# Queries of the cross attention laid out in DRAM as a group's tile has them, loaded by three DMAs a group and stored by three a tile

## The reference, cut to what matters

```python
def _L0_xattn_ref(query, key, value, masked, Wq, Wk, Wv, Wo):     # query: x of shape (4, 1024, 256); key, value: context (4, 77, 256)
    q = split_heads(query @ Wq)                                    # 16 heads of 16
    k = split_heads(key @ Wk)
    v = split_heads(value @ Wv)
    scores = jnp.einsum('bhqd,bhkd->bhqk', q, k) * scale
    scores = jnp.where(masked[:, None, :, :], NEG, scores)
    attn = jax.nn.softmax(scores, axis=-1)
    out = jnp.einsum('bhqk,bhkd->bhqd', attn, v)
    return out.transpose(0, 2, 1, 3).reshape(query.shape[0], -1, EMBED_DIM) @ Wo
```

## Time and profile before

| | us |
|---|---|
| three runs | 1057.42, 1067.87, 1074.19 |
| median | 1067.87 |
| the profiled execution | 1068.38 |
| its span, first to last instruction | 1066.7 |

### The profile page before, as it was taken

One profiled execution on the slowest core, in us unless ns is written; L12 is line 12 of the kernel. 1 busy time (PEld: TensorE's weight loads), 2 busy tenths in 40 slices (PEclk: granted clock), 3 DMA queues, 4 the chain that ended last, 5 costly groups with the idle time before them and its releaser, 6 DMA issues.

```text
span 1066.7 us, 19077 instructions
## 1 busy us (share of the span) xinstructions
PE 1025.8 (96%) x7059; PEld 603.9 (57%) x7108; DVE 722.7 (68%) x1603; ACT 577.6 (54%) x1093; POOL 198.3 (19%) x220
## 2 busy tenths in 40 slices
PE   5999999999999999999999999899999999999998
PEld 4877344444444444444444466444544588888887
DVE  7878887787887787877785387646566365555552
ACT  4785276676766676676675667457556411111110
POOL 6655000000000000000000034101000033333331
PEclk9999699999999999999999999869999999999999
DMA  8696903444443334444400048758673100000001
GB/s 259 207 280 209 177 6 78 82 82 82 82 69 60 65 64 78 86 85 82 81 14 19 10 122 185 174 89 159 117 130 61 33 8 21 20 21 20 20 21 40
DMA packets 82202, 93.27 MB, mean 87 GB/s; under 512 B 14676, under 2 KB 75312, under 8 KB 80573
## 3 DMA queue, kind: packets, MB, share of 16 engines
q1 hardware_dynamic: 79527, 88.85, 38.3%
q10 hardware_dynamic: 2582, 3.20, 1.4%
HBM read 53.55 MB, written 28.80 MB: 77 GB/s over the span
## 4 chain that ended last, share of the span: by engine, by line
PE 77%; DVE 14%; ACT 3%; issue 2%; DMA 2%; SPq 1%; POOL 0%; POOLq 0%; DVEq 0%; ACTq 0%
PE bank L134 20%; PE bank L870 12%; PE bank L837 11%; PE bank L856 9%; DVE pm L767 7%; PE bank L1544 3%; PE bank L1440 3%; PE bank L1430 2%; PE bank L1432 2%; PE bank L1141 2%; PE bank L968 2%; PE bank L860 2%; PE bank L1413 2%; PE bank L842 2%; PE bank L1415 1%
## 5 line engine op out<-in xcount | busy, mean ns | idle before, releaser
L767 DVE TENSOR_REDUCE pm<-bank 128x1 f32<-128x512 f32 (+3 forms) x608 | 356.9, 654 | 86.6 <-PE bank L842 65.6
L814 ACT ACTIVATE prob<-bank 128x512 f32<-128x512 f32 (+1 forms) x608 | 317.5, 584 | 174.0 <-PE bank L860 87.9
L837 PE MATMUL bank<-stk,stq 96*128 96x512 bf16 (+3 forms) x768 | 224.4, 336 | 5.6 <-DVE pm L767 3.2
L856 PE MATMUL bank<-stq,stk 98*128 98x512 bf16 (+3 forms) x768 | 221.5, 328 | 2.7 <-ACT prob L814 0.7
L870 PE MATMUL bank<-prob,va 128*17 128x512 f32 (+3 forms) x1536 | 145.0, 496 | 2.7
L837 PEld LDWEIGHTS bank<-stk,stq 96*128 96x128 bf16 x768 | 68.3, 98 | 134.9 <-DVE pm L767 76.8
L1692 ACT ACTIVATE e_sg<-bank 128x512 f32<-128x512 f32 x48 | 28.7, 598 | 174.4 <-PE bank L134 172.3
L1379 ACT ACTIVATE xprob<-bank 80x512 f32<-80x512 f32 x128 | 73.0, 592 | 73.8 <-PE bank L1432 70.8
L753 POOL TENSOR_TENSOR xres<-xres,bo_b 128x256 f32<-128x256 f32 x32 | 23.2, 724 | 399.2 <-DVE pm L767 204.2
L856 PEld LDWEIGHTS bank<-stq,stk 98*128 98x128 bf16 x768 | 69.1, 98 | 44.7 <-ACT prob L814 9.1
L1609 POOL TENSOR_TENSOR e_ht<-e_hf,e_ht 128x512 fp32r<-128x512 f32 x48 | 62.2, 1296 | 109.9 <-DVE e_ht L1634 109.8
(11 more groups left out here) (183 smaller groups left out, 1354.6 us busy)
## 6 DMA issues: line engine op xcount, KB each, us to landing
qk<-a_parts SPq DMA_DIRECT2D x32, 384.0 KB, 2.8
xq<-c_parts SPq DMA_DIRECT2D x16, 384.0 KB, 2.7
xstq<-xq SPq DMA_DIRECT2D x32, 192.0 KB, 4.2
stq<-qk SPq DMA_DIRECT2D x30, 192.0 KB, 3.9
stk<-qk SPq DMA_DIRECT2D x15, 384.0 KB, 6.4
vs<-a_vst SPq DMA_DIRECT2D x8, 544.0 KB, 3.8
oall<-u_out SPq DMA_DIRECT2D x64, 64.0 KB
xstq<-xq SPq DMA_DIRECT2D x32, 128.0 KB, 4.5
```

The costliest lines, as they stand in the source:

```text
L767: nc.vector.tensor_reduce(pm[:, k, h0:h0 + hb, r], src[:, 0:hb * w].rearrange("p (h w) -> p h w", h=hb), AX, ALU.max).then_inc(s_mxe, 1)
L814: nc.scalar.activation(prob[:, U % NPS, 0:hb * n], bank[STB[U % NSB]][:, 0:hb * n], ACT.Exp).then_inc(s_ex, 1)
L837: mm = nc.tensor.matmul(dst[:, h * w:(h + 1) * w], stq[i][0:R, half, h0 + h, r * P:(r + 1) * P], stk[i][0:R, h0 + h, k0:k0 + w], start=(h ...
L856: mm = nc.tensor.matmul(dst[:, h * n:(h + 1) * n], stk[i][0:RM, h0 + h, kt * P:(kt + 1) * P], stq[i][0:RM, half, h0 + h, q0:q0 + n], start ...
```

## The change

`xq3` gets the order that a group's tile has: for a batch, a half of the features, a part and a number r of the head there are two groups, and for a group 2 halves x 4 heads x 512 queries lie together, 8 KB in one piece. Before, a head's 1,024 queries lay together (2 KB). A load then takes one piece of 8 KB for each partition, and three DMAs fill a tile. The stored tile's rows no longer share one stride for all partitions and parts, so each part has a DMA of its own. The numbers that the semaphores are waited for follow.

```diff
-    xq3 = dram("xq3", (B, KT, 3, P, S), BF16)
+    xq3 = dram("xq3", (B, KT, 3, HD, HP // HG, 2, HG, CH), BF16)
...
                 sp.wait_ge(cs_lo, KT * c + n + 1)
-                sp.dma_start(xq3[b, n, :, :, u * CH:(u + 1) * CH].rearrange("c p s -> p c s"),
-                             cparts[:, u, n]).then_inc(cso[u], 16)
+                for part in range(3):
+                    sp.dma_start(xq3[b, n, part, :, :, u].rearrange("r a h s -> (r a) h s"),
+                                 cparts[:, u, n, part]).then_inc(cso[u], 16)
...
-                        sp.wait_ge(cso[w], 16 * KT)
+                        sp.wait_ge(cso[w], 48 * KT)
                     load_cross(sp, c - 2)
             for w in range(2):
-                sp.wait_ge(cso[w], 16 * KT * B)
+                sp.wait_ge(cso[w], 48 * KT * B)
...
-                need(a, cso[c % 2], 16 * KT * (c // 2))
+                need(a, cso[c % 2], 48 * KT * (c // 2))
...
             for slot, first, number in Q_RUNS:
-                for c in range(2):
-                    sp.dma_start(xstq[i][HD * slot:HD * (slot + number), c],
-                                 xq3[b, i // 2, first:first + number, :, c * 512:(c + 1) * 512]
-                                 .rearrange("c (r h) s -> (c r) h s", h=HP)
-                                 [:, HG * (i % 2):HG * (i % 2 + 1)]).then_inc(xld[i], 16)
+                sp.dma_start(xstq[i][HD * slot:HD * (slot + number)].rearrange("p u h q -> p (u h q)"),
+                             xq3[b, i // 2, first:first + number].rearrange("c r a u h s -> (c r) a (u h s)")
+                             [:, i % 2]).then_inc(xld[i], 16)
...
-                    t.wait_ge(xld[i], 32 * len(Q_RUNS) * (b + 1))
+                    t.wait_ge(xld[i], 16 * len(Q_RUNS) * (b + 1))
```

## The result

The changed kernel took 1067.94 us, the median of 21 runs (1062.14 to 1075.17). The kernel before, in 21 runs beside it, had 1061.04 (20 of them between 1057.42 and 1074.23; one of 3491.92 doesn't move the median). The ratio is 1.0059, with a 95% interval of 1.0042 to 1.0076: slower by 0.6%, about 6 us, clear of noise and well inside 2%. The forecast of 1068 us with "no change beyond 2%" holds. That the figure was hit is luck, two errors that cancel: I added 0.1 us to a median of three runs, 1067.87, that stood 7 us above what more runs of the same kernel give, and the change cost about 6 us.

The account below looks back on a forecast made before the run. TensorE bounds the kernel (77% of the span); DMA waits with the low clock offer 13.5 us. +0.1 (last store) + 0 (earlier stores, issue, bytes, group 7) on 1068.38 gives 1068.5, forecast 1068 us; range 1055 to 1080 for 8 in 10.

Parts of the forecast that it names:

- no change beyond 2%: Whole kernel: time stays within about 2% (21 us) of the kernel before, given 93 in 100.
- the bytes of the loads: Query loads: 8 KB runs flow no faster than 1 KB runs; 0 us, ends 2.2 less and 1.2 more.
- Rival (a): Query loads flow faster in long runs, 2.2 us less; idle time and low clock go, 1055 us; 6 in 100.
- Rival (c): Long-run query loads flow slower, 1.2 us more each, 1082 us; with one further low stretch, 1080, together 12 in 100.
- (d): Query loads: the 8 KB runs are cut into short packets again; only SP's issue time is saved, 1068 us.
- the place: Cross stage: TensorE's 2.1 us wait for group 1's maxima row; with the low clock behind it 13.5 us to win.
- the last store: Last query store before group 3's load: third part issued at 676.02, landing at 677.8 to 678.6; +0.1 us.
- a store that ends later holds up nobody: Stores before the last: 12 us more of SP's issue time fits into its 33.4 us of waiting; 0 us.
- The low clock stays: Behind group 1's wait: the 24 us low stretch, costing 11.4 us, remains, as idle time goes from 2.07 to about 2.2 us.
- Rival (b): Clock falls for a shorter time or not at all, with waits as they are; 1057 us; 22 in 100.
- group 7: Group 7's load behind 768 KB of `up_t`, TensorE idle 0.69 us: no change, 0 us, ends -0.7 and +1.2.
- over 1 us at group 7: Sign that the forecast is wrong: a wait for `xstq` of over 1 us at group 7 or later.

Follow-up runs that it names:

- loads3: Kernel before with only the loads changed: three loads a group, 8 KB runs, one store a tile as before; 1059.57 us, ratio 0.9986.
- stores3_flat: Kernel before with only the stores changed: three a tile, old order in DRAM, 128 rows each; 1063.07 us, ratio 1.0028.
- early_after: Changed kernel with group 1's maxima row sent ahead of the wait for the last stores and of group 3's load; 1059.75 us, ratio 0.9992.
- the 67 runs: Later runs of the unchanged kernel before, beside the experiments, two slow ones of 69 left out; on average 1061.4 us.
- base: Kernel before once more, no edit, with every run's granted clock on record; 1058.35 us, ratio 0.9982.
- early_before: Kernel before with only group 1's maxima row sent ahead of the wait for the last stores and of group 3's load; 1059.29 us, ratio 0.9975.
- delay3: Kernel before plus three spare stores of 32 x 4 rows issued between the wait for the last stores and group 3's load; 1063.09 us, ratio 1.0045.
- early_weights: Kernel before with the early maxima row, and `up_t` and `down_t` issued behind a group's query load; 1057.36 us, ratio 0.9982.

## Why the prediction was right, and which steps were wrong

**Right: the bytes of the loads.** Long runs flow as fast as short ones. In the change, group 3's load is first issued at 679.85 and its last 128 KB, issued at about 680.7, landed 6.1 us later:

```profile
xstq<-xq SPq DMA_DIRECT2D x1, 128.0 KB, 6.1
```

That is 6.9 us from first issue to last landing, against 6.7 before and "6 to 7" forecast; `loads3` puts it alone and finds 0.9986. The self-attention stage was the right place to read this price. Rival (a) falls: no run shows a joined load landing sooner. The Trainium skill, page "DMA: Bandwidth & Descriptors", section on rules for kernel authors, speaks for joining small transfers, and the page's fit, which it gives for transfers issued from GpSimd, made an estimated 3.8 us of it; the measured 6.9 us decide against both here. Rival (c), slower long runs, falls too, and (d) by the packets.

**Right: the place.** In the change the only wait for these DMAs of more than 0.5 us is the maxima row of group 1, and it lands at about the end of group 3's load when it is issued behind it, 1.4 us earlier or not.

**Wrong: the last store, "+0.1 us, with the ends 0 and +0.75".** The load started 1.85 us later, and the idle time became 3.44 us where about 2.2 was forecast. The step took 0.376 us an issue, the median of stores that SP issues alone with time before them, and put the third part at 675.27 + 0.75 = 676.02. Issued one behind another they take 0.602 each, with the gaps about 3.9 us for the six of a chunk; the last chunk's six ran from 673.88 to 678.18, one of them taking 1.16 us, and the last started at 677.57, 1.55 us later than I had it. From the last tile's first part, at 676.28, to the load it took 3.6 us, not about 2.8. The last store's landing was priced too low as well, 2.1 us and not 1.8 (1.8 is what the stores of `stores3_flat` took, with 128 rows). Two rows ahead of the prediction spoke for it: the three sends in 2.55 us and the four stores of sums in 2.46 us are issues of 0.6 us or more, which I had only counted as such. The upper end failed by the same step, since it varied the landing and not the issue.

**Wrong: "a store that ends later holds up nobody".** In the waits after, ScalarE waited for one, and SP's slack fell from 33.4 us to 17.5:

```profile
SPq L1020 <- POOL c_parts L1041: 17.5, 7, 8.3
...
ACT c_parts L1101 <- DMA xq<-c_parts: 1.5, 1, 1.5
```

It cost TensorE nothing that `early_after` shows, which has the same stores and a ratio of 0.9992.

**Wrong in size: the price of the idle time.** "The low clock stays" took its 24 us from one execution. Over the 67 runs the time at the low clock varies from 13 us to 45 for the same kernel, so a longer wait shifts how often and how long the clock falls: 10 us more on average. The 1.4 us lost at the full clock and 0.47 x 10.0 = 4.7 us by the low clock are the 6 us. The idle time in the change's profile is 1.4 us longer than in that of before and 2.4 longer than in that of `base`, so how the 1.4 us come about is shown to no better than 1 us. Rival (b), a shorter or absent low stretch, at 1057, has its mechanism in the runs of before, whose median lies 7 us under the profiled execution; I gave it 22 in 100 for the change and should have asked it of the base. Of group 7, as forecast, little came in the change's profile: 0.5 us of wait. In other profiles this wait is 0.69 us (before), 1.29 (`base`), 1.33 (`early_before`) and 2.83 (`stores3_flat`), so the sign "over 1 us at group 7" would have come up without the change too.

## What to carry to other kernels

Count the issues of a queue, and price one by rows where they stand back to back and have the shape at hand: joining 96 loads into 48 won nothing, since the bytes set their end, while splitting 16 stores into 48 kept SP issuing for 2 us longer ahead of its one urgent transfer. A small row that the tensor engine waits for goes ahead of a bulk load in the same queue, as soon as its data are ready. And where the clock reacts to idle time, take the base from the clocks of many runs, not from one profile or a median of three.

## What the runs showed of the hardware

- SP's issue of a store: 0.36 to 0.38 us for a lone one of 384 KB; for those of 128 KB with 128 rows against 128 partitions 0.32 to 0.34 at the head of a row of issues and 0.448 in the median of 48; as 32 x 4 rows against 128 partitions 0.52 and 0.602. In both kernels with 48 stores single issues took 0.75 to 1.16 us (at 671 and 674 to 675); why is open.
- Behind the same load, issued at the same times within 0.11 us, the row of 8 KB let TensorE start at 685.35 in one run and at 684.42 in another.
- The granted clock behind the wait at group 1, by its length, one profile each: 1.02 us (twice), 1.00; 2.07, low for 23.9 us; 2.31, 3.26, 3.44 and 4.08, low for 10.2 us each. Further on, from 690 to 740, waits of 1.89 to 2.07 us for VectorE had a low stretch of 3.4 to 10.2 us behind or around them (the change, `loads3`, `early_after`), waits of 1.33 and 2.83 us for a query load one of 3.4 and 6.8 (`early_before`, `stores3_flat`), and waits of 1.00 and 1.29 (`base`), 0.79 (`delay3`) and 1.02 us (`early_weights`) none.
- One us at the low clock cost 0.47 us of time in 67 runs of the kernel before, against 11.4 / 24 = 0.475 worked out ahead from two groups.
- Loads of 768 KB into 96 partitions took 6.7 us from first issue to last landing in runs of 1 KB and 6.7 to 6.9 in runs of 8 KB; that the partitions set this rate was argued from the 128-partition rows, and no run tried it.
